# A router's scores with its weights as the fixed operand, in an FFN-attention-FFN kernel

## What is computed

```python
x = x + 0.5 * ffn(layernorm(x))
x = x + attention(layernorm(x))      # 16 heads, causal
x = x + 0.5 * ffn(layernorm(x))

def ffn(x):
    weights = golden_weights(x, Wr, temperature)      # 8 experts, from x @ Wr
    h = silu(einsum('btd,edf->betf', x, Wg)) * einsum('btd,edf->betf', x, Wu)
    return einsum('bte,betd->btd', weights, einsum('betf,efd->betd', h, Wd))
```

## Time and profile before

| | |
|---|---|
| median of 3 runs | 757.83 us (757.0 to 759.11) |
| the profiled execution | 756.76 us, of which the span of the instructions is 755.0 us |
| busy | PE 744.4 us, PEld 596.8, DVE 478.3, ACT 346.3, POOL 417.9 |
| chain that ended last | PE 92% |
| granted TensorE clock | 9 tenths or more of full speed (2.4 GHz) in all 40 slices |

### The profile page before, as it was taken

The page is one execution under the profiler, slowest core; times in us unless marked ns, Lnnn a source line. Parts: engine busy times, 40 slices in busy tenths (PEclk is TensorE's granted clock), DMA queues, the critical chain, the costliest instruction groups (busy, mean ns, idle before and its releaser), DMA issues.

```text
span 755.0 us, 13968 instructions
## 1 busy us (share of the span) xinstructions
PE 744.4 (99%) x4782; PEld 596.8 (79%) x4782; DVE 478.3 (63%) x1308; ACT 346.3 (46%) x657; POOL 417.9 (55%) x497
## 2 busy tenths in 40 slices
PE   7999999999999999999999999999999999999998
PEld 6788889877788677778777778777777788888887
DVE  6968856865567757688456766865657632574333
ACT  4555336344465444656445456454353552332322
POOL 4595674554763445754555753554564655556663
PEclk9999999999999999999999999999999999999999
DMA  9354423643234534225542413535322333223231
GB/s 296 118 175 147 141 84 96 192 134 104 94 98 130 161 114 124 81 82 148 153 122 90 145 64 113 157 116 175 93 83 89 95 103 113 85 71 127 98 111 57
DMA packets 69719, 90.22 MB, mean 119 GB/s; under 512 B 13200, under 2 KB 49424, under 8 KB 69648
## 3 DMA queue, kind: packets, MB, share of 16 engines
q1 hardware_dynamic: 67456, 89.01, 37.8%
q10 hardware_dynamic: 2192, 0.32, 0.2%
HBM read 72.10 MB, written 17.04 MB: 118 GB/s over the span
## 4 chain that ended last, share of the span: by engine, by line
PE 92%; SPq 2%; DMA 2%; DVE 2%; issue 1%; ACT 0%; POOL 0%; DVEq 0%
PE ra L777 15%; PE ra L778 15%; PE ra L779 15%; PE dn L799 8%; PE dn L800 8%; PE dn L801 8%; PE ra L882 5%; PE ra L909 5%; PE ra L897 4%; PE ra L754 2%; SPq L1461 1%; PE ra L851 1%; PE ra L853 1%; PE ra L864 1%; PE ra L866 1%; PE ra L852 1%
## 5 line engine op out<-in xcount | busy, mean ns | idle before, releaser
L1378 POOL TENSOR_TENSOR hid<-hid,wb 128x512 f32<-128x512 f32 x124 | 163.8, 1322 | 155.9 <-DVE hid L1237 152.0
L1382 POOL TENSOR_TENSOR ht_lo<-hid,ht_hi 128x512 fp32r<-128x512 f32 x124 | 161.3, 1302 | 119.0 <-ACT ht_hi L1015 118.7
L777 PE MATMUL ra<-xt_hi,wgu_hi 128*128 128x512 f32 x512 | 225.6, 441 | 0.4 <-DVE mx L1288 0.3
L778 PE MATMUL ra<-xt_hi,wgu_lo 128*128 128x512 f32 x512 | 202.3, 395 | 0.0
L779 PE MATMUL ra<-xt_lo,wgu_hi 128*128 128x512 f32 x512 | 201.8, 394 | 0.0
L1288 DVE CUSTOM_DVE_ANT_0 junk<-ra,mask 128x128 bf16<-128x128 f32 (+3 forms) x256 | 121.3, 486 | 85.0 <-PE ra L882 83.5
L799 PE MATMUL dn<-wd,ht_hi 128*128 128x256 f32 x512 | 160.9, 314 | 0.0
L1229 DVE SCALAR_TENSOR_TENSOR hid<-hid,ra 128x512 f32<-128x512 f32 x125 | 85.8, 686 | 110.2 <-ACT hid L1007 109.6
L800 PE MATMUL dn<-wd,ht_hi 128*128 128x256 f32 x512 | 144.0, 281 | 0.0
L801 PE MATMUL dn<-wd,ht_lo 128*128 128x256 f32 x512 | 143.9, 281 | 0.0
L1015 ACT ACTIVATE ht_hi<-hid 128x512 fp32r<-128x512 f32 x124 | 78.0, 629 | 122.8 <-POOL hid L1378 103.1
(11 more groups left out here) (160 smaller groups left out, 839.8 us busy)
## 6 DMA issues: line engine op xcount, KB each, us to landing
wd<-wd_parts SPq DMA_DIRECT2D x56, 512.0 KB, 3.7
wb<-wts_rows SPq DMA_DIRECT2D x62, 256.0 KB, 3.8
qk_parts<-parts SPq DMA_DIRECT2D x32, 192.0 KB, 2.1
q_st<-qk_parts SPq DMA_DIRECT2D x96, 64.0 KB, 2.5
k_st<-qk_parts SPq DMA_DIRECT2D x96, 64.0 KB, 2.2
wd_parts<-wd SPq DMA_DIRECT2D x8, 512.0 KB, 3.7
ctx_rows<-cx SPq DMA_DIRECT2D x16, 256.0 KB, 2.5
stage<-in_Wg SPq DMA_DIRECT2D x8, 256.0 KB, 4.5
```

The source lines that it names most:

```text
L777: mm(b_, w_hi, xt_hi[q % 2][:, c, :], start=c == 0, stop=False)
L778: mm(b_, w_lo, xt_hi[q % 2][:, c, :], start=False, stop=False)
L1378: nc.gpsimd.tensor_tensor(tb, tb, wb[m % NWB][:, :], ALU.mult).then_inc(hw_done, 1)
L1382: nc.gpsimd.tensor_tensor(ht_lo[n % NHT][:, :], hidden(n)[:, :], f32(ht_hi[n % NHT][:, :]), ALU.subtract).then_inc(lo_done, 1)
```

## The change

The fixed operand of the router's matmuls becomes `wr`, widened with zeros from 16 to 72 columns; the tokens move through, 512 at a time. That leaves the scores as 72 rows by 512 tokens, so a second item, `zt`, is needed: ACT copies the rows to SBUF (over `xn[0]`), and PE transposes them back in four pieces. `bias` on DVE is cut into two items (`bl` makes the low part of bv, `bias` adds the product). In the planner the low parts of `sg` 2 and `sd` 1 come after the last route piece of block 0, and DVE's `small` after `ln` 0 1.

```diff
-CONSTS = 7
+CONSTS = 8
+ZC = 72
...
-        put(start + 3.5, ("z", q))
+        put(start + 3.3, ("z", q))
+        put(start + 3.6, ("zt", q))
...
         add(low[0][0], ("sg", e), 2.4 if low[0][0] == "pool" else 1.15, ("act", "sg", e), port=True,
-            then=[("dve", "ln", 0, 1)] if e == 0 else [])
+            then=[("dve", "ln", 0, 1)] if e == 0 else [("dve", "route", 0, ROUTE_PIECES - 1)] if e == 2 else [])
...
         add(low[1][0], ("sd", e), 1.25 if low[1][0] == "pool" else 0.6, ("act", "sd", e), port=True,
-            then=[("dve", "xt", 0, 1)] if e == 0 else [])
+            then=[("dve", "xt", 0, 1)] if e == 0 else [("dve", "route", 0, ROUTE_PIECES - 1)] if e == 1 else [])
...
-    add("dve", ("bias",), 1.0, ("act", "bias"), ("pe", "bias"))
-    add("pe", ("bias",), 0.71, ("act", "bias"), ("dve", "sa", 1), more=0.8)
+    add("dve", ("bl",), 1.4, ("act", "bias"), port=True)
+    add("dve", ("bias",), 0.45, ("pe", "bias"))
+    add("pe", ("bias",), 0.71, ("dve", "bl"), ("dve", "sa", 1))
...
-        add("pe", ("z", q), 1.8, ("dve", "xt", q, 0), ("dve", "xt", q, 1), ("dve", "small"))
-        add("dve", ("z", q), 0.22, ("pe", "z", q), ("act", "route", q - 1, 0) if q else None)
-        add("act", ("route", q, 0), 0.25, ("dve", "z", q))
+        both = ("dve", "xt", q, 1) if q else ("act", "xt", q, 1)
+        add("pe", ("z", q), 0.95 if q else 1.2, both, ("dve", "small"))
+        add("act", ("z", q), 0.6, ("pe", "z", q), holds=("xn", 0))
+        add("pe", ("zt", q), 0.45, ("act", "z", q), lets=("xn", 0))
+        add("dve", ("zt", q), 0.25, ("pe", "zt", q), ("act", "route", q - 1, 0) if q else None)
+        add("act", ("route", q, 0), 0.25, ("dve", "zt", q))
...
                         pe.wait_ge(r_lo, 1)
-                        for i in range(QT):
-                            if i % 2 == 0:
-                                pe.wait_ge(*emptied(("xt", q, i // 2)))
-                            b_, tok = o[:, i * 2 * E:(i + 1) * 2 * E], slice(i * P, (i + 1) * P)
-                            for c in range(KT):
-                                mm(b_, xt_hi[q % 2][:, c, tok], wr[:, c, :], start=c == 0, stop=False)
-                                last = mm(b_, xt_lo[q % 2][:, c, tok], wr[:, c, :], start=False, stop=c == KT - 1)
+                        pe.wait_ge(xhi_done, 2 * q + 2)
+                        for k, rows in enumerate((xt_hi[q % 2], xt_lo[q % 2])):
+                            if k == 1:
+                                for m in range(2):
+                                    pe.wait_ge(*emptied(("xt", q, m)))
+                            for c in range(KT):
+                                last = mm(o[0:ZC, :], wr[:, c, :], rows[:, c, :], start=k + c == 0, stop=k + c == KT)
+                        last.then_inc(ra_full, 1)
+                    if kind == "zt":
+                        pe.wait_ge(*emptied(("z", it[1])))
+                        for i in range(QT):
+                            last = nc.tensor.transpose(o[:, i * P:i * P + ZC], z_rows[0:ZC, i * P:(i + 1) * P], ident[0:ZC, 0:ZC])
                         last.then_inc(ra_full, 1)
...
+                    if kind == "z":
+                        if it in XN_BEFORE:
+                            act.wait_ge(ra_full, full(XN_BEFORE[it]))
+                        nc.scalar.activation(z_rows[0:ZC, :], o[0:ZC, :], ACT.Copy).then_inc(freed, 1)
...
+                chain(nc.gpsimd.memset(stage_r[:, :, E:ZC], 0.0))
```

More of the change, by code:

```diff
@@ L125, in schedule @@
     put(-9.47, ("small",))
+    put(16.8, ("bl",))
     put(17.8, ("bias",))
@@ L129, in schedule @@
     put(-8.0, ("z", 0))
+    put(-7.9, ("zt", 0))
     put(1.60, ("wbp", 0))
@@ L210, in schedule @@
     return {it: t for t, it in at}
-RING = ("bias", "xt", "z", "wbp", "wt", "x", "qk", "v", "max", "mt", "exp", "pv", "wo")
-FREED_BY = {k: "act" for k in ("wbp", "wt", "v", "exp", "pv")} | {
-    k: "dve" for k in ("bias", "xt", "x", "z", "qk", "max", "mt", "wo")}
+RING = ("bias", "xt", "z", "zt", "wbp", "wt", "x", "qk", "v", "max", "mt", "exp", "pv", "wo")
+FREED_BY = {k: "act" for k in ("z", "wbp", "wt", "v", "exp", "pv")} | {
+    k: "dve" for k in ("bias", "xt", "x", "zt", "qk", "max", "mt", "wo")}
 FIRST = {"dve": {"t": -1.0, "h": -1.0, "max": 0.0, "sg": 0.0, "sd": 0.0, "stats": -0.2, "route": -0.5},
@@ L343, in routed @@
     def routed(q):
-        return ("dve", "z", q)
+        return ("pe", "zt", q)
     p = Plan(target)
@@ L376, in plan @@
     add("act", ("small",), 1.4)
-    add("dve", ("small",), 0.5, ("act", "small"))
+    add("dve", ("small",), 0.5, ("act", "small"), then=[("dve", "ln", 0, 1)])
     add("pe", ("warm",), 0.42 * WARM, ("sp", "ldx", 0))
     add("act", ("bias",), 0.7, ("pool", "lo", NHID - 1))
-    add("dve", ("bias",), 1.0, ("act", "bias"), ("pe", "bias"))
-    add("pe", ("bias",), 0.71, ("act", "bias"), ("dve", "sa", 1), more=0.8)
+    add("dve", ("bl",), 1.4, ("act", "bias"), port=True)
+    add("dve", ("bias",), 0.45, ("pe", "bias"))
+    add("pe", ("bias",), 0.71, ("dve", "bl"), ("dve", "sa", 1))
     for n in range(NCH):
@@ L554, in build @@
         for it in ACT_ORDER:
[L555 to L558, removed]
+            if it[0] in ("ln", "aln", "z") and it != ("ln", 0, 1):
+                m = it[2] if it[0] != "z" else 0
+                if m in latest:
+                    XN_BEFORE[it] = latest[m]
+                elif m == 1:
                     XN_BEFORE[it] = ("xt", 0, 1)
-                latest[it[2]] = ("xt" if it[0] == "ln" else "x",) + it[1:]
+                latest[m] = ({"ln": "xt", "aln": "x", "z": "zt"}[it[0]],) + it[1:]
         x_res = sb("x_res", [P, NT, D])
@@ L632, in build @@
         stage = [over(f"stage{i}", [P, KT, 3 * D], F32, probs_at + 6144 * i) for i in range(NSTAGE)]
-        stage_r = over("stage_r", [P, KT, E], F32, x2_at + 5120)
+        stage_r = over("stage_r", [P, KT, ZC], F32, x2_at + 5120)
         first_hid = [over("hid_a", [P, T], F32, cx_at), over("hid_b", [P, T], F32, cn_at),
@@ L929, in _ @@
                         o, freed = rbank(it), ra_free[BANK[it]]
-                    if kind in ("xt", "wbp", "wt", "x", "qk", "v", "mt", "exp", "pv"):
+                    if kind in ("xt", "z", "wbp", "wt", "x", "qk", "v", "mt", "exp", "pv"):
                         act.wait_ge(ra_full, full(it))
@@ L933, in _ @@
                         act.wait_ge(wr_in, 32)
-                        nc.scalar.activation(wr[:, :, 0:E], stage_r[:, :, :], ACT.Copy).then_inc(r_hi, 1)
                         act.wait_ge(consts, CONSTS)
+                        nc.scalar.activation(wr[:, :, :], stage_r[:, :, :], ACT.Copy).then_inc(r_hi, 1)
                         for c in range(2):
@@ L1142, in _ @@
                         nc.vector.tensor_scalar(half_rt[:, :], half_rt[:, :], 0.5, None, ALU.mult).then_inc(rt_done, 1)
-                    if kind == "bias":
+                    if kind == "bl":
                         dve.wait_ge(bv_done, 1)
@@ L1148, in _ @@
                         ins.then_inc(bv_done, 1)
+                    if kind == "bias":
                         dve.wait_ge(ra_full, full(it))
@@ L1218, in _ @@
                                                 f32(xt_hi[q % 2][:, :, half]), ALU.subtract).then_inc(freed, 1)
-                    if kind == "z":
+                    if kind == "zt":
                         dve.wait_ge(ra_full, full(it))
-                        nc.vector.tensor_reduce(out=z[a3], in_=o[:, 0:QT * 2 * E].rearrange("p (i s e) -> p i e s", i=QT, s=2),
+                        nc.vector.tensor_reduce(out=z[a3],
+                                                in_=o[:, :].rearrange("p (i r) -> p i r", i=QT)[:, :, 0:2 * E]
+                                                .rearrange("p i (s e) -> p i e s", s=2),
                                                 axis=AX.X, op=ALU.add).then_inc(freed, 1)
```

9 lines of the change are left out of this document (5 added, 4 removed).

## The result

| | before | after |
|---|---|---|
| median | 757.9 us (757.0 to 759.1, 5 runs) | 754.2 us (753.8 to 754.8, 5 runs) |
| the profiled execution | 756.76 us, span 755.0 | 754.57 us, span 752.8 |

The ratio is 0.9956, with a 95% interval from 0.9944 to 0.9968: faster by 3.3 us (2.4 to 4.2), clear of no change. The forecast was 754.0.

A forecast was written before the change was run, and what follows sets the result against it. PE was taken as the bound, busy 744.4 of 755.0 us. Savings of 0.85 at the start and 2.95 in blocks 1 to 7 gave 753.0, plus 1.07 to the median: 754.0 us, range 752.0 to 757.3.

The forecast's parts named there:

- The products: In each block's new scores, four matmuls of 512 moving columns at 0.23 us each, 0.93 us in all.
- The transposes: In each block's new scores, four transposes at 0.11 us each, 0.44 us in all; upper bound 1.02.
- The term for the seven blocks: Blocks 1 to 7: scores cost PE 1.37 us instead of 1.79, 0.42 saved in each, 2.95 us in all.
- The sign: In the profile after the change, busy PE falls by about 3 us.
- Block 0: At the start, PE begins the spread of the first experts' weights (L837, now L852) 0.85 us earlier.
- all just in time: Behind the first spread of weights, `wbp` 1, `wt` 0 and `g` 3 start at 25.1, 26.0 and 26.1 us.
- POOL holds the route off: First route operation in block 0 waits for POOL's second low part, so the route starts only 0.28 us earlier.
- The edits at nothing: `bl` and `bias`, ACT's copies, later `small`, wider `wr` and later `sd` 1 low part were costed at nothing.
- the loss of this cover: At `bl` and `bias`: with DVE's 277 us to spare gone, PE would wait one DVE operation, 0.68 us.
- PE waits in the attention: Rival: PE waits at `zt` or at reordered attention items, taking back 2 to 4 us, 756 to 758; chance 0.16.
- The sum: Whole kernel: 0.85 + 2.95 = 3.8 us saved, profiled execution 753.0, median 754.0 us.
- the step from its profile to the median: Median of the runs before, 757.83 us, lies 1.07 above the profiled execution, 756.76; added to the forecast.

The follow-up runs named there:

- the second profile: Profile of the changed kernel run once more, unedited: 753.98 us, ratio 0.9946.
- the rest alone: Changed kernel with the old router put back, keeping the cut of `bias` and the three order rules: 759.06 us, ratio 1.0015.
- the router alone: Kernel before with only the router's new form (`z`, `zt`, 72 columns), `bias` uncut, old planner rules: 759.51 us, ratio 1.0015.
- twice the transposes: Changed kernel with the four transposes of every block done twice: 755.05 us, ratio 0.9959.
- the second copy: Changed kernel run again, unedited, beside other edited kernels on the same chip: 754.07 us, ratio 0.9959.
- width 64: Changed kernel with the router's fixed operand 64 columns wide instead of 72: 756.21 us, ratio 0.9982.

## Why the prediction was right

- **The products**: 0.23 us each forecast, 0.23 measured, at 32, 64 and 72 columns alike.
- **The transposes** are the term that was mis-sized: 0.44 us for four were forecast from transposes of 128 rows, 0.30 were measured. The sentence that nothing spoke for less than 0.44 was wrong. The term for the seven blocks is 4.0 us instead of 2.95. The sign went with it: busy PE fell by 5.2 us, not by about 3.
- **Block 0**: L852 0.85 us earlier forecast, 0.88 measured at equal landing. The steps hold one by one when 0.58 (the later load) is taken off the second profile: `g` 0 at 14.22 (14.17), the first route operation done at 18.87 (18.96), L852 at 24.18 (24.21), and then a wait of 1.1 (1.2). The step behind it, "all just in time", was a little off: `g` 3 came only 0.73 us earlier.
- **POOL holds the route off**, so that the rules gain only what DVE's operation took from POOL's: forecast 0.28, measured 0.47. Taking POOL's part away gave the rest.
- **The edits at nothing.** The cut of `bias` cost nothing, but without it the new order loses 3.0 us of waiting and some 1.7 of clock. The prediction priced the loss of this cover at one operation, 0.68 us; it is seven times that.
- **PE waits in the attention** stood as a rival with 2 to 4 us. Part of it came: waits of 0.4 to 1.2 us at L764 and L912 that were not there before. From `g` 3 on the profiles are 3.4 and 3.2 us shorter instead of 4.0, so the net price is 0.6 to 0.8 us. The waits of over 0.1 us behind `g` 3 add up to 2.1 and 2.3 us for 0.3 before, more than that net price, so other steps became some 1.2 us shorter; which, the runs don't tell. At `zt` there is no wait, but it was close, as forecast: in block 1 ACT's copy ends 0.16 us before `zt` starts (0.1 was worked out), in the other blocks 0.24 to 1.3.
- **The sum**: 4.0 + 0.73 - 0.7 = 4.0 us by the profiles at equal landing of the load, 3.8 forecast, 3.4 to 3.7 by the medians. That the forecast is met so closely is partly luck. The cheaper transposes (1.05) and the dearer attention (0.7) nearly cancelled, and two things were not in the sum at all: the loads that land about 0.5 us later, and the clock, which falls less often than before. The prediction added 1.07 us for the step from its profile to the median as if both kernels lost the same; at a like clock the gain is 2.9 us.

Left open: why the attention's new order needs more of DVE's and the loads' time in general (only the wait for `den` was tried), why the first loads land later, and why the clock falls less often.

## What to carry to other kernels

Cost a group of matmuls by the distance of starts with its neighbours, not by durations, and look at how many rows a small one uses: just over 64 was cheaper than 64 or 32. An order written by a planner carries its covers with it: a new form of one item can pull another item ahead of its operand, and the wait of 3 us on PE cost half as much again in clock. When POOL holds DVE off, try moving POOL's work as well as DVE's: here one gave 1.3 us at `g` 3, the other 0.3. Look at the granted clock of all executions, not only of the profiled one, before comparing medians.

## What the runs showed of the hardware

- A transpose of 72 rows costs 0.063 us in a row of its kind, and four with their edges 0.30; of 64 or 32 rows four cost 0.58 and 0.56.
- Two small DVE operations took 1.73 us beside POOL, and one took 1.79 where it takes 0.17 alone.
- The clock at the start does not follow from the length of one wait. It fell to 1.2 GHz in the kernel with the rest alone (idle for 2.04 and then 1.07 us; low for 6.8 us), in the first profile of the changed kernel (2.03 and 1.55; 3.4 us), with the router alone (1.30 and 1.51) and with twice the transposes (1.20 and 1.59). It stayed at 2.4 GHz before (0.15 and 1.13), in the second copy (1.85 and 1.31) and at width 64 (1.96 and 1.19). What decides was not tried.
